# Attention on one core: the first 128 columns of W_Q and W_K split ahead of the rest, the first batch's context loaded into the accumulator, and three x transposes moved into the V products

## The chip, the cores and the metric

The kernel runs on one core of a Trainium2 chip. The metric is the device time of one execution in microseconds, here the median of three runs. A core has five engines that run side by side and meet through semaphores: TensorE (PE in the profile, its weight loads PEld), VectorE (DVE), ScalarE (ACT), GpSimd (POOL) and SyncE (SP), which here issues every DMA.

## The reference

Two layers of gated attention and feed-forward work over x of 8 batches of 512 rows by 512 columns, in float32. Only the first part, the attention of layer 0, is touched:

```
q = layernorm(x) @ W_Q + b_Q ; k = ctx @ W_K + b_K ; v = ctx @ W_V + b_V     (16 heads of 32)
out = softmax(q k^T / sqrt(32)) v ;  x = x + tanh(g) * (out @ W_O + b_O)
```

After it come a feed-forward part with ternary weights (their codes are made during the attention), a second attention without projections, and a product with block-quantised weights (W_ffn of layer 1, quantised during the attention too).

## The kernel before

All of the change is in `attention_phase`. Each engine runs its own instruction list. The lists come from one clock: steps are entered with a tick (`ck.add(tick, rank, name, ...)`), a batch has 640 ticks, and every engine walks the steps in the order of their ticks (ACT and DVE with small extra delays by kind of step), unrolled over the 8 batches. A tick sets the order only; the time is set by what waits for what.

A batch has 4 groups of 160 ticks, one for each 4 heads. A group is 16 slots of 8 ticks, then a burst. In a slot PE does one `max` product (a query tile's scores, of which DVE takes the row maximum, L870) and one `score` product (scores again, with the maximum's row appended, of which ACT takes the exponential, L751). In the burst PE does the 16 products with V (`pv`, L643) and the column sums (`den`, L662); then DVE takes four reciprocals (`recip`, L881) and the normalised output (L886), in the slots of the next group. PE may run at most two `max` products ahead of DVE.

Between these go the fillers, which make the next batch ready:

- `t`: a tile of normalised x or of the context is transposed on PE (four 128x128 transposes, L566); ACT writes a rounded high part (L701), then DVE the low part (L845). x goes to `xt`, the context to `ct`. Tiles 0 to 3 are x, tiles 4 to 7 the context.
- `qk`: four chunks of three products for one group of 128 columns and one side (Q or K), L582, then ACT (L714) and DVE (L857) write the two parts with the bias. `spill` and `fill` carry them by DMA to the layout of `stack`; the part of group 0's K goes there directly.
- `v`: sixteen chunks of three products (L596) in the slots of a batch's own group 0, and ACT reads out each of the four results (L735).

The results of `t`, `qk` and `v` share two PSUM banks, `work`, which go round in the order of the ticks (`Turns`): each user waits until the user before the last has been read out.

Before, `tx_at = (0, 1.5, 3, 4.5)` and `tc_at = (10.8, 12.3, 13.8, 15.3)` put all eight transposes into group 1 (slots counted from its start), the chunks of `(0, Q)` at slots 6 to 9.45 of it, and those of `(0, K)` at 16.8 to 20.25, which is the start of group 2. A context tile is loaded into the `stage` slot that its x tile leaves, six ticks after that tile's transposes.

At the start SP loads four x tiles, then all of W_Q, the biases, all of W_K, later W_V. Each weight is written as a high part by ACT (`split_weight`, L671) and a low part by DVE (L825), 2048 elements per partition in one instruction each, W_Q's on ACT between the third and the fourth normalisation (L723). W_V's low part is made by POOL (`ones_row`, L939). The block quantisation of the layer 1 weight is a series of steps on DVE (`quantise`, L797 to L819).

Of the kernel before, what the change touches and what calls it, by code (L numbers as in the profile page):

```python
# [5 lines left out]
ALU = mybir.AluOpType  # L6
# [3 lines left out]
P = 128  # L10
# [167 lines left out]
def attention_phase(nc, NB, keep0, keep1, x, ctx_in, w_q, b_q, w_k, b_k, w_v, b_v, spill, attn_t, ctx_t, ffn_w, w_o, b_o, weight, delta_w,  # L178
# [54 lines left out]
    with ExitStack() as ctx:  # L233
# [14 lines left out]
        def permuted(n, h):  # L248

            to = w["qkv"[n]][:, :, h, :]  # L250
            src = probs[:, n].rearrange("p a b -> p (a b)").rearrange("p (c e) -> p c e", c=C)
            if n == 2:
                return to, src
            return (to.rearrange("p c (g r j) -> p c g r j", g=G, j=J), src.rearrange("p c (g j r) -> p c g r j", g=G, j=J))
# [36 lines left out]
        w_loaded, w_hi, w_lo = [sem(f"w_loaded_{n}") for n in "qkv"], sem("w_hi"), sem("w_lo")  # L291
        wv_lo, bias_put, bias_turned, bias_done, ln_nmean = sem("wv_lo"), sem("bias_put"), sem("bias_turned"), sem("bias_done"), sem("ln_nmean")
        consts, bias_loaded, pool_consts = sem("consts"), sem("bias_loaded"), sem("pool_consts")
        loaded = [sem(f"loaded{i}") for i in range(STAGE)]
# [126 lines left out]
        def stage_wait(engine, it, shift, i):  # L421
            wait_count(engine, loaded[i % STAGE], it, shift, 2 * T // STAGE, i // STAGE + 1, 16)

        with nc.Block() as block:
            @block.sync
            def _(sp):
# [10 lines left out]
                def load_weight(n, src):  # L437
                    sp.dma_start(probs[:, n], src.rearrange("(c p) e -> p c e", p=P)).then_inc(w_loaded[n], 16)

                def window(it, shift, name, args):  # L440
                    b = it + shift
                    if name == "load":
                        i, = args
                        sync_wait(sp, held, t_full, it, shift, 2 * T, i - STAGE + 1)
                        src = x if i < T else ctx_in
                        sp.dma_start(stage[:, i % STAGE, :], src[bass.ds(b, 1), (i % T) * P:(i % T + 1) * P, :])\
                            .then_inc(loaded[i % STAGE], 16)
# [91 lines left out]
            def _(pe):  # L539
# [15 lines left out]
                def window(it, shift, name, args):  # L555
                    if name == "t":
# [8 lines left out]
                        for c in range(C):  # L565
                            last = nc.tensor.transpose(turns.bank("t", i)[:, c * P:(c + 1) * P],  # L566
                                                       stage[:, i % STAGE, c * P:(c + 1) * P], ident[:])
                        last.then_inc(t_full, 1)
                    elif name == "qk":
                        g, side, c = args  # L570
                        if c == 0:
                            if isinstance(it, int) and it + shift == 0 and g == 0:
                                pe.wait_ge(w_hi, side + 1)
                                pe.wait_ge(w_lo, side + 1)
# [11 lines left out]
                    elif name == "v":  # L586
                        i, c = args
                        if c == 0:
                            if isinstance(it, int) and it + shift == 0 and i == 0:
                                pe.wait_ge(w_hi, 3)  # L590
# [76 lines left out]
            def _(act):  # L667
                def split_weight(n):
                    act.wait_ge(w_loaded[n], 16)
                    to, at_n = permuted(n, HI)  # L670
                    nc.scalar.activation(to, at_n, ACT.Copy).then_inc(w_hi, 1)  # L671
# [17 lines left out]
                def window(it, shift, name, args):  # L689
                    if name == "t":  # L690
# [12 lines left out]
                        if isinstance(it, int) and it + shift == 0 and i == T - 1:  # L703
                            put_biases()
                            split_weight(1)
                    elif name == "qk" and args[2] == C - 1:
# [9 lines left out]
                        if isinstance(it, int) and it + shift == 0 and g == 0 and side == K:  # L716
                            split_weight(2)
                            small_tables()
                    elif name == "norm":
# [5 lines left out]
                        if isinstance(it, int) and it + shift == 0 and i == T - 2:  # L725
                            split_weight(0)
                        if it + shift == 0 and i == T - 1:
                            act.wait_ge(bias_loaded, 48)
                            nc.scalar.activation(bpart[:].rearrange("n (r j) -> n r j", j=J), brow[:].rearrange("n (j r) -> n r j", j=J),
                                                 ACT.Copy).then_inc(bias_put, 1)  # L730
# [51 lines left out]
            def _(dve):  # L782
# [39 lines left out]
                def split_weight(n):  # L822
                    dve.wait_ge(w_hi, n + 1)
                    (to, at_n), (high, _) = permuted(n, LO), permuted(n, HI)
                    nc.vector.tensor_tensor(to, at_n, high.bitcast(F32), ALU.subtract).then_inc(w_lo, 1)  # L825

                def window(it, shift, name, args):
                    if name == "ln1":
# [9 lines left out]
                        if isinstance(it, int) and it + shift == 0 and i == T - 1:  # L838
                            split_weight(0)
                    elif name == "t":  # L840
# [6 lines left out]
                        if isinstance(it, int) and it + shift == 0 and i == T - 1:  # L847
                            split_weight(1)
                            dve.wait_ge(bias_done, 2)
                        if it + shift == 0 and i == 2 * T - 1:  # L850
# [3 lines left out]
                    elif name == "qk" and args[2] == C - 1:  # L854
                        g, side, _ = args
                        wait_count(dve, qk_hi, it, shift, 2 * G, 2 * g + side + 1)
                        nc.vector.scalar_tensor_tensor(part[:, side, LO, :], turns.bank("qk", g, side)[:], bias[:, side, g:g + 1],  # L857
                                                       part[:, side, HI, :].bitcast(F32), ALU.add, ALU.subtract).then_inc(qk_lo, 1)
# [67 lines left out]
            def _(pool):  # L926
# [7 lines left out]
                def ones_row():  # L934
# [3 lines left out]
                    pool.wait_ge(w_hi, 3)  # L938
# [901 lines left out]
```

## Time and profile before

| | us |
|---|---|
| runs | 1613.11 median, 1610.33 to 1617.53 |
| profiled execution, its own time | 1618.44 |
| its span | 1616.7 |
| first `max` product starts | 50.40 |
| burst of batch 0, group 0 (its `den`) | 103.78 |
| last burst of the attention (its `den`) | 837.07 |

Times in rows are microseconds from the start of the span. In a timeline row stand start, duration, engine, line, operation, tiles, shapes and count, and in brackets the idle time of the engine just before, with what ended it. A window row has its bounds, its length and each engine's busy time with its count; the windows here run from one group's `den` to the next, and the sum is over the seven groups 1 that have all their fillers. Matmul durations overlap: the distance from one start to the next is what a matmul costs in a dense stretch.

### The profile page before, as it was taken

What the parts mean: (1) busy time and instruction counts of PE and PEld (TensorE: products, weight loads), DVE (VectorE), ACT (ScalarE), POOL (GpSimd) and SP (SyncE); (2) the same over time, 40 slices, a digit from 0 to 9 for tenths busy, and PEclk for the clock granted to TensorE, in tenths of its full rate; (3) what the DMA queues carried; (4) which work ended last, traced back from release to release, by engine and by line L of the source; (5) the groups of instructions that cost most, each with busy time, mean ns of one, the idle gap of its engine ahead of it and who ended that gap; (6) DMA issues with size and microseconds to landing.
All of it is one profiled execution on the core that took longest, in us unless ns stands there. A gap on an engine that the chain in (4) does not pass through costs nothing. (4 is left out here: it accounts for less than half of the span.)

```text
span 1616.7 us, 24697 instructions
## 1 busy us (share of the span) xinstructions
PE 1479.7 (92%) x6994; PEld 939.2 (58%) x6994; DVE 1229.8 (76%) x2135; ACT 879.3 (54%) x1435; POOL 887.7 (55%) x1148
## 2 busy tenths in 40 slices
PE   4789989999999999999784999999999978999997
PEld 3565666566665565666432555555555447787785
DVE  4867687677778778786552788888888848999996
ACT  4256666666566565665442555555555535565552
POOL 2166766675775756755552343343334316777775
PEclk8889999999999989999777999999999989999998
DMA  5666858586694875957932344444444743556521
GB/s 189 170 208 182 245 160 237 170 231 193 164 275 141 223 221 145 280 137 209 268 79 62 92 113 111 108 107 107 107 110 107 192 144 125 163 167 206 165 86 62
DMA packets 233868, 261.13 MB, mean 162 GB/s; under 512 B 139804, under 2 KB 162856, under 8 KB 224040
## 3 DMA queue, kind: packets, MB, share of 16 engines
q1 hardware_dynamic: 233768, 259.95, 57.3%
q8 instruction: 44, 0.72, 0.2%
q14 instruction: 56, 0.46, 0.1%
HBM read 143.20 MB, written 78.68 MB: 137 GB/s over the span
## 5 line engine op out<-in xcount | busy, mean ns | idle before, releaser
L751 ACT ACTIVATE a_probs<-a_sc 128x512 f32<-128x512 f32 x512 | 300.3, 595 | 277.4 <-PE a_sc L624 275.3
L870 DVE TENSOR_REDUCE a_negmax<-a_mx 128x1 f32<-128x512 f32 x512 | 337.8, 674 | 96.4 <-PE a_mx L607 95.8
L965 POOL TENSOR_TENSOR a_acc<-a_acc,a_probs 128x512 f32<-128x512 f32 x248 | 311.5, 1285 | 10.6 <-ACT a_probs L751 9.4
L965 POOL TENSOR_TENSOR a_acc<-a_probs 128x512 f32<-128x512 f32 x124 | 156.8, 1284 | 239.6 <-ACT a_probs L751 238.8
L607 PE MATMUL a_mx<-a_stack 96*128 96x512 f32 x512 | 230.2, 450 | 38.5 <-DVE a_negmax L870 23.4
L1116 PE MATMUL bank<-wcode,b_xq 128*128 128x512 bf16 x1024 | 229.8, 383 | 11.1 <-DMA b_xq<-b_xcode 11.1
L624 PE MATMUL a_sc<-a_stack 97*128 97x512 f32 x512 | 215.7, 423 | 11.1 <-DMA a_stack<-a_mrow 9.7
L1116 PEld LDWEIGHTS bank<-wcode,b_xq 128*128 128x128 bf16 x1024 | 100.9, 99 | 135.2 <-DMA b_xq<-b_xcode 12.4
L881 DVE RECIPROCAL a_attn<-a_den 128x128 f32<-128x128 f32 x128 | 120.7, 947 | 72.4 <-PE a_den L662 57.1
L607 PEld LDWEIGHTS a_mx<-a_stack 96*128 96x128 f32 x512 | 102.7, 201 | 113.8 <-DVE a_negmax L870 57.9
L1154 ACT ACTIVATE b_sig<-bank,b_tok 128x512 f32<-128x512 f32 x128 | 87.4, 683 | 94.5 <-PE bank L1116 91.4
L582 PE MATMUL a_work<-a_xt,k_wbuf 128*128 128x512 f32 x384 | 123.6, 437 | 12.0 <-DVE a_xt L845 12.0
L1208 DVE TENSOR_TENSOR b_hid<-b_sig,bank 128x512 f32<-128x512 f32 x128 | 87.4, 685 | 51.3 <-ACT b_sig L1154 51.3
L624 PEld LDWEIGHTS a_sc<-a_stack 97*128 97x128 f32 x512 | 103.2, 202 | 37.8 <-DMA a_stack<-a_mrow 10.0
L643 PE MATMUL a_pvb<-a_probs,a_v 128*32 128x512 f32 x1024 | 119.9, 607 | 0.7 <-ACT a_probs L751 0.7
L1158 ACT ACTIVATE b_hid<-b_hid,b_htok 128x2048 f32<-128x2048 f32 x32 | 64.1, 2003 | 102.9 <-DVE b_htok L1227 102.9
L582 PE MATMUL a_work<-k_wo,k_wbuf 128*128 128x512 f32 x384 | 115.1, 412 | 1.5 <-DVE k_wo L845 1.5
L1105 PE MATMUL bank<-k_wo,b_apart 128*128 128x512 f32 x384 | 102.6, 417 | 14.9 <-POOL b_apart L1259 13.9
L1123 PE MATMUL bank<-wcode,b_hq 128*128 128x512 bf16 x512 | 116.1, 380 | 0.0
L596 PE MATMUL a_work<-k_wbuf,k_wo 128*128 128x512 f32 x384 | 111.2, 401 | 0.0
L1530 PE MATMUL bank<-c_ct,c_xt 128*128 128x512 f32 x384 | 98.9, 407 | 11.1 <-DVE c_xt L1628 8.8
L582 PEld LDWEIGHTS a_work<-a_xt,k_wbuf 128*128 128x128 f32 x384 | 80.9, 214 | 35.1 <-issue 14.2
(169 smaller groups left out, 2573.5 us busy)
## 6 DMA issues: line engine op xcount, KB each, us to landing
a_stack<-spill SPq DMA_DIRECT2D x168, 256.0 KB, 7.2
spill<-k_part SPq DMA_DIRECT2D x56, 512.0 KB, 3.4
ctx_t<-k_wo SPq DMA_DIRECT2D x16, 1024.0 KB, 11.1
c_ct<-ctx_t SPq DMA_DIRECT2D x8, 2048.0 KB, 8.2
a_stage<-in_x_dram SPq DMA_DIRECT2D x32, 256.0 KB, 5.1
a_stage<-in_ctx_dram SPq DMA_DIRECT2D x32, 256.0 KB, 3.3
a_wsum<-in_L_ffn_w_gate_dram SPq DMA_DIRECT2D x8, 1024.0 KB, 5.9
attn_t<-a_attn SPq DMA_DIRECT2D x32, 256.0 KB, 4.5
```

Of the source, the lines that this page charges most:

```text
L582: last = nc.tensor.matmul(turns.bank("qk", g, side)[:], w["qk"[side]][:, c, a, g * P:(g + 1) * P], src[:, c, m, :], start=c == 0 and n == ...
L596: last = nc.tensor.matmul(turns.bank("v", i)[:], ct[:, c, a, i * P:(i + 1) * P], w["v"][:, c, m, :], start=c == 0 and n == 0, stop=c == C ...
L607: nc.tensor.matmul(mx[i % 2][:], stack[0:96, g, Q, j, t * P:(t + 1) * P], stack[0:96, g, K, j, :], start=True, stop=True).then_inc(mx_full, 1)
L624: nc.tensor.matmul(sc[i % 2][:], stack[0:97, g, K, j, k * P:(k + 1) * P], stack[0:97, g, Q, j, :], start=True, stop=True).then_inc(s_full, 1)
L643: last = nc.tensor.matmul(pvb[DH * j:DH * (j + 1), :], v[:, k, h * DH:(h + 1) * DH], probs[:, k, j, :], start=k == 0, stop=k == T - 1)
L751: nc.scalar.activation(probs[:, k, j, :], sc[i % 2][:], ACT.Exp, scale=SCALE).then_inc(exp_done, 1)
L870: nc.vector.tensor_reduce(negmax[:, g % 2, j, t:t + 1], mx[i % 2][:], axis=AX.X, op=ALU.max, negate=True).then_inc(mx_done, 1)
L881: nc.vector.reciprocal(attn[:, g % 2, q * P:(q + 1) * P], den[:, q * P:(q + 1) * P]).then_inc(recip_done, 1)
L965: nc.gpsimd.tensor_tensor(acc[:, j], probs[:, 0, j] if k == 1 else acc[:, j], probs[:, k, j], ALU.add)\
L1105: last = nc.tensor.matmul(bank_o[:], apart[:, t % 2, a, c, :], wo[:, c, m, :], start=c == 0 and n == 0, stop=c == C - 1 and n == 2)
L1116: last = nc.tensor.matmul(bank[:], xq[:, t % 2, c, :], gu_code[:, side * M + m, :, c, :], start=c == 0, stop=c == C - 1)
L1123: last = nc.tensor.matmul(bank_d[:], hq[:, t % 2, r, :], wcode[:, 2 * M:3 * M, r, :], start=r == 0, stop=r == R - 1)
```

## The change

What it does:

1. `tx_at` becomes (-7.25, -3.5, -0.5, 0.3): x tiles 0 to 2 are transposed in the slots of group 0, at ticks 70, 100 and 124 of it, between the V chunks, and tile 3 at tick 2 of group 1. The loads of the context follow by six ticks.
2. `(0, Q)` moves to slots 2.6 to 6.05 of group 1, the context transposes to 7.5, 9, 10.5 and 12, and `(0, K)` to 13.4 to 16.85: three of its four chunks come ahead of the burst of group 1. The fills of group 0 move from slots 17 and 22.8 to 16 and 19.4.
3. The first batch's context tiles are loaded into `acc` (not in use by then), without waiting for `stage`.
4. W_Q and W_K are loaded and split in two parts, columns 0 to 127 (all that group 0 needs) and 128 to 511, the latter in four instructions of 384 elements per partition on ACT and on DVE. The order at the start changes: no split stands between the normalisations any more.
5. The first quantisation steps (`quantise` 0 to 2) move on DVE from the last context tile to the K part of group 0, behind the split of the rest of W_K.

```diff
+        SPLIT_AT = (1, 2, 2 + C, 2 + 2 * C, 3 + 2 * C)
+        def pieces(n, h, cols):
+            to, src = w["qkv"[n]][:, :, h, cols], staged(n, cols)
             if n == 2:
-                return to, src
+                return [(to, src)]
+            to, src = to.rearrange("p c (g r j) -> p c g r j", r=DH, j=J), src.rearrange("p c (g j r) -> p c g r j", r=DH, j=J)
+            if cols.stop == P:
+                return [(to[:, :, 0], src[:, :, 0])]
+            return [(to[:, c], src[:, c]) for c in range(C)]
...
-        tx_at, tc_at = (0, 1.5, 3, 4.5), (10.8, 12.3, 13.8, 15.3)
-        qk_at = {(0, Q): 6, (0, K): 16.8, (1, Q): 21.4, (1, K): 26, (2, Q): 30.6, (2, K): 35.2, (3, Q): 39.8, (3, K): 44.4}
-        fill_at = {(0, Q): 17, (0, K): 22.8, (1, Q): 32, (1, K): 37, (2, Q): 44.5, (2, K): 49.5, (3, Q): 52, (3, K): 56}
+        tx_at, tc_at = (-7.25, -3.5, -0.5, 0.3), (7.5, 9, 10.5, 12)
+        qk_at = {(0, Q): 2.6, (0, K): 13.4, (1, Q): 21.4, (1, K): 26, (2, Q): 30.6, (2, K): 35.2, (3, Q): 39.8, (3, K): 44.4}
+        fill_at = {(0, Q): 16, (0, K): 19.4, (1, Q): 32, (1, K): 37, (2, Q): 44.5, (2, K): 49.5, (3, Q): 52, (3, K): 56}
@@ SP, load @@
-                        sync_wait(sp, held, t_full, it, shift, 2 * T, i - STAGE + 1)
+                        to = stage[:, i % STAGE, :]
+                        if b == 0 and i >= T:
+                            to = acc[:, i - T, :]
+                        else:
+                            sync_wait(sp, held, t_full, it, shift, 2 * T, i - STAGE + 1)
...
-                        if isinstance(it, int) and b == 0 and i == T - 1:
-                            load_weight(0, w_q)
+                        if b == 0 and i == T - 1:
+                            load_weight(0, w_q, slice(0, P), w_first[0])
                             load_biases()
-                            load_weight(1, w_k)
-                        if isinstance(it, int) and b == 0 and i == 2 * T - 1:
+                        if b == 0 and i == 2 * T - 1:
+                            load_weight(1, w_k, slice(0, P), w_first[1])
+                            load_weight(0, w_q, slice(P, D))
+                            load_weight(1, w_k, slice(P, D))
                             load_weight(2, w_v)
@@ ACT, t @@
-                        if isinstance(it, int) and it + shift == 0 and i == T - 1:
+                        if it + shift == 0 and i == 1:
+                            split_weight(0, True)
+                        if it + shift == 0 and i == T - 2:
+                            act.wait_ge(bias_loaded, 48)
+                            nc.scalar.activation(bpart[:].rearrange("n (r j) -> n r j", j=J), brow[:].rearrange("n (j r) -> n r j", j=J),
+                                                 ACT.Copy).then_inc(bias_put, 1)
+                        if it + shift == 0 and i == T - 1:
                             put_biases()
-                            split_weight(1)
+                        if it + shift == 0 and i == 2 * T - 2:
+                            split_weight(1, True)
+                        if it + shift == 0 and i == 2 * T - 1:
+                            split_weight(0, False)
@@ ACT, qk @@
-                        if isinstance(it, int) and it + shift == 0 and g == 0 and side == K:
-                            split_weight(2)
+                        if it + shift == 0 and g == 0 and side == K:
+                            split_weight(1, False)
+                            split_weight(2, False)
                             small_tables()
@@ DVE, qk; its low parts of the splits stand at the same tiles as ACT's high parts @@
+                        if it + shift == 0 and (g, side) == (0, K):
+                            split_weight(1, False)
+                        if it + shift == 0 and (g, side) == (0, K):
                             dve.wait_ge(q_loaded, 16)
                             for n in range(3):
                                 quantise(n)
```

## Rows read from the trace of the kernel before

**Rows 1.** The page: busy time, share and instructions of each engine.

```profile
PE 1479.7 (92%) x6994; PEld 939.2 (58%) x6994; DVE 1229.8 (76%) x2135; ACT 879.3 (54%) x1435; POOL 887.7 (55%) x1148
```

**Rows 2.** Group 1 windows: busy PE, PEld, DVE, ACT, POOL; clock, DMA share, GB/s.

```profile
199.98:224.87 24.89, 21.62 (x121) 13.52 (x117) 19.34 (x30) 16.18 (x31) 15.07 (x12) 0.93 0.35 117
...
sum 182.16, PE 159.77 PEld 100.24 DVE 145.75 ACT 112.43 POOL 105.36; mean PE 22.82 PEld 14.32 DVE 20.82 ACT 16.06 POOL 15.05
```

**Rows 3.** Window, same columns: the group 0 before it, `den` to `den`.

```profile
176.53:199.98 23.45, 23.45 (x126) 16.27 (x122) 14.58 (x21) 15.36 (x28) 16.20 (x16) 1.00 0.90 270
```

**Rows 4.** Waits of PE, 100 to 780 us: total, times, longest.

```profile
PE a_mx L607 <- issue: 9.6, 10, 1.7
```

**Rows 5.** Timeline of PE in one group 1.

```profile
200.95 0.66 PE L566 MATMUL a_work<-k_ident,a_stage 128*128 128x128 f32 x4
201.36 0.48 PE L607 MATMUL a_mx<-a_stack 96*128 96x512 f32 x1
...
205.91 0.50 PE L607 MATMUL a_mx<-a_stack 96*128 96x512 f32 x1 [1.27 <-DVE a_negmax L870]
...
209.19 0.94 PE L582 MATMUL a_work<-a_xt,k_wbuf 128*128 128x512 f32 x3 [1.64 <-DVE a_xt L845]
...
212.23 0.63 PE L607 MATMUL a_mx<-a_stack 96*128 96x512 f32 x1
```

**Rows 6.** Timeline of DVE in the same group.

```profile
206.96 0.95 DVE L881 RECIPROCAL a_attn<-a_den 128x128 f32<-128x128 f32 x1
...
207.83 0.63 DVE L870 TENSOR_REDUCE a_negmax<-a_mx 128x1 f32<-128x512 f32 x1
...
208.37 0.68 DVE L845 TENSOR_TENSOR a_xt<-a_work,a_xt 128x512 fp32r<-128x512 f32 x1
208.96 0.69 DVE L870 TENSOR_REDUCE a_negmax<-a_mx 128x1 f32<-128x512 f32 x1
```

**Rows 7.** Timeline of the end of a group 0, ACT and PE.

```profile
191.38 0.60 ACT L735 ACTIVATE a_v<-a_work 128x512 f32<-128x512 f32 x1
...
191.65 1.55 PE L596 MATMUL a_work<-k_wbuf,k_wo 128*128 128x512 f32 x6
...
196.52 3.64 PE L643 MATMUL a_pvb<-a_probs,a_v 128*32 128x512 f32 x32
...
196.81 0.57 ACT L735 ACTIVATE a_v<-a_work 128x512 f32<-128x512 f32 x1
```

**Rows 8.** Timeline of group 2, SP and PE.

```profile
232.93 1.94 SPq L480 DMA_DIRECT2D a_stack<-k_part  x3
...
241.12 0.47 PE L607 MATMUL a_mx<-a_stack 96*128 96x512 f32 x1 [0.81 <-issue]
```

**Rows 9.** Timeline of the start, all engines.

```profile
9.44 0.19 POOL L955 TENSOR_TENSOR a_nbias<-a_nmean,a_rstd 128x1 f32<-128x1 f32 x1
...
9.87 3.77 ACT L671 ACTIVATE k_wbuf<-a_probs 128x2048 fp32r<-128x2048 f32 x1 [0.18 <-DMA a_probs<-in_L_xattn_W_Q_dram]
...
22.12 5.03 PE L582 MATMUL a_work<-a_xt,k_wbuf 128*128 128x512 f32 x12 [1.50 <-DVE a_xt L845]
...
34.88 2.28 DVE L797 TENSOR_REDUCE a_attn<-a_wsum 128x64 f32<-128x2048 f32 x1
...
41.20 0.75 DVE L857 SCALAR_TENSOR_TENSOR k_part<-a_work,a_bias,k_part 128x512 fp32r<-128x512 f32 x1 [3.59 <-ACT k_part L714]
42.11 2.02 SPq L480 DMA_DIRECT2D a_stack<-k_part  x3
...
43.12 4.55 POOL L939 TENSOR_TENSOR k_wbuf<-a_probs,k_wbuf 128x2048 fp32r<-128x2048 f32 x1 [26.50 <-ACT k_wbuf L671]
...
44.96 2.78 DVE L803 SCALAR_TENSOR_TENSOR a_attn<-a_attn 128x64 f32<-128x64 f32 x1
...
50.40 0.76 PE L607 MATMUL a_mx<-a_stack 96*128 96x512 f32 x1 [5.09 <-DMA a_stack<-k_part]
...
51.20 0.69 DVE L870 TENSOR_REDUCE a_negmax<-a_mx 128x1 f32<-128x512 f32 x1 [0.54 <-PE a_mx L607]
```

More of the change, by code:

```diff
@@ L289, in attention_phase @@
         pvb, den = pb("pvb"), pb("den")
[L291 removed]
+        w_loaded, w_first, w_hi, w_lo = [sem(f"w_loaded_{n}") for n in "qkv"], [sem(f"w_first_{n}") for n in "qk"], sem("w_hi"), sem("w_lo")
         wv_lo, bias_put, bias_turned, bias_done, ln_nmean = sem("wv_lo"), sem("bias_put"), sem("bias_turned"), sem("bias_done"), sem("ln_nmean")
         consts, bias_loaded, pool_consts = sem("consts"), sem("bias_loaded"), sem("pool_consts")
[L294 removed]
+        loaded, ctx_first = [sem(f"loaded{i}") for i in range(STAGE)], [sem(f"ctx_first{i}") for i in range(T)]
         ln_stats, ln_mv, ln_eps, ln_rstd, ln_bias, ln_done = (sem(n) for n in ("ln_stats", "ln_mv", "ln_eps", "ln_rstd", "ln_bias",
@@ L421, in stage_wait @@
         def stage_wait(engine, it, shift, i):
-            wait_count(engine, loaded[i % STAGE], it, shift, 2 * T // STAGE, i // STAGE + 1, 16)
+            b = it + shift
+            if b == 0 and i >= T:
+                engine.wait_ge(ctx_first[i - T], 16)
+            else:
+                engine.wait_ge(loaded[i % STAGE], 16 * (2 * b + i // T + (b == 0)))
         with nc.Block() as block:
@@ L565, in window @@
                         for c in range(C):
-                            last = nc.tensor.transpose(turns.bank("t", i)[:, c * P:(c + 1) * P],
-                                                       stage[:, i % STAGE, c * P:(c + 1) * P], ident[:])
+                            tile = acc[:, i - T] if it + shift == 0 and i >= T else stage[:, i % STAGE]
+                            last = nc.tensor.transpose(turns.bank("t", i)[:, c * P:(c + 1) * P], tile[:, c * P:(c + 1) * P], ident[:])
                         last.then_inc(t_full, 1)
@@ L571, in window @@
                         if c == 0:
-                            if isinstance(it, int) and it + shift == 0 and g == 0:
-                                pe.wait_ge(w_hi, side + 1)
-                                pe.wait_ge(w_lo, side + 1)
+                            if it + shift == 0 and g <= 1:
+                                pe.wait_ge(w_hi, SPLIT_AT[2 * g + side])
+                                pe.wait_ge(w_lo, SPLIT_AT[2 * g + side])
+                            if it + shift == 0 and g == 0:
                                 pe.wait_ge(bias_done, 2)
@@ L667, in _, with split_weight @@
             def _(act):
[L668 to L671, printed above, removed]
+                def split_weight(n, first):
+                    cols = slice(0, P) if first else slice(P, D)
+                    if n == 2:
+                        cols = slice(0, D)
+                    act.wait_ge(w_first[n] if first else w_loaded[n], 16)
+                    for to, at_n in pieces(n, HI, cols):
+                        nc.scalar.activation(to, at_n, ACT.Copy).then_inc(w_hi, 1)
                 def small_tables():
@@ L724, in window @@
                                              bias=nbias[:, i:i + 1]).then_inc(ln_done, 1)
[L725 to L730, printed above, removed]
                     elif name == "v" and args[1] == C - 1:
@@ L820, in quantise, with split_weight @@
                     ins.then_inc(q_step, 1)
[L822 to L825, printed above, removed]
+                def split_weight(n, first):
+                    dve.wait_ge(w_hi, SPLIT_AT[n if first else n + 2])
+                    cols = slice(0, P) if first else slice(P, D)
+                    for (to, at_n), (high, _) in zip(pieces(n, LO, cols), pieces(n, HI, cols)):
+                        nc.vector.tensor_tensor(to, at_n, high.bitcast(F32), ALU.subtract).then_inc(w_lo, 1)
                 def window(it, shift, name, args):
@@ L853, in window @@
                                 quantise(n)
[L854 to L858, printed above, removed]
                         if it + shift == 0 and (g, side) == (1, Q):
```

36 lines of the change are left out of this document (21 added, 15 removed).

## The prediction

> **What bounds the kernel now.** The page first: PE is busy 92% of the span, DVE 76% [rows 1], so time is lost where PE waits, and I looked for that inside the attention (to 837 us). The windows by group come next. A group 0, with sixteen V chunks, takes 23.45 us with PE busy for all of them at full clock [rows 3]: PE bound. A group 1 takes 24.89 us at best and 182.16 / 7 = 26.0 us on average, though it has fewer chunks, with PE busy 22.8 of 26.0 and DVE 20.8 [rows 2]. The timelines say why. All eight tiles' low parts, four reciprocals and sixteen row maxima go through DVE; PE waits 1.27 us for a maximum and 1.64 us for the last x tile [rows 5], and soon after that the products last 0.63 us: the granted clock falls to 1.2 GHz. At a mean clock of 0.93 that is 2 x 0.07 x 24.89 = 3.5 us at the lower level, which costs 1.7 us if PE is busy throughout; it isn't quite, and I take 1.5. Without it this group 1 would take 24.89 - 1.5 = 23.4, so the seven lose 26.0 - 23.4 = 2.6 us each, mostly to the clock. Each group 2 has a wait of 0.8 us for the fill of K's group 0, seven such among the ten of [rows 4], one in [rows 8].
>
> So x and the first Q chunks are a real stall; the question is whether moving them ends it, and what it costs in group 0, where PE has nothing to spare.
>
> **Group 0: what is added.** Three tiles' transposes move in. One costs PE 201.36 - 200.95 = 0.4 us [rows 5], and there is no cover: 1.2 us. Then the two banks. With x tile 0 between V2 and V3, V3 now takes the bank of V2 and waits for ACT to read it. V2's read-out is 191.38 to 191.98, and V3's first chunk started at 191.65 [rows 7]: with the semaphore 0.4 us late. x tile 2 (tick 124) takes the bank of V3, and all of the burst is queued behind it. V3 is read out only from 196.81 to 197.38, behind the maximum's row and an exponential on ACT, while the burst started at 196.52 [rows 7]: 0.9 us late. Sum: 1.2 + 0.4 + 0.9 = +2.5 us. Bounds: +1.2 (the read-outs come earlier) to +3.0. ACT and DVE take these tiles inside PE's 1.17 us slots and in the burst, where DVE is idle: nothing.
>
> **Group 1: what goes and what replaces it.** DVE works back to back here, at intervals of 207.83 - 206.96 = 0.87 us for a reciprocal, 0.54 to 0.6 for a maximum, 0.6 for a low part [rows 6]. In the new order the low part of context tile 7 stands behind 4 reciprocals (3.5), 13 maxima (7.8), 4 other low parts and itself (3.0), Q's part (0.65) and the output (0.6): 15.6, with 0.4 of start and gap makes 16.0 us after the burst. `(0, K)` can't start before. Then come three chunks at 0.7, two slots at 0.47 and the row of maxima's transpose at 0.2: 19.3 us to the next burst. Before it was 221.41 - 200.95 = 20.5 with the clock's 1.5 in it, 19.0 without. So with the same loss by the clock: +0.3. The stall moves from Q behind x to K behind the context.
>
> Does the clock still fall? Before, in the 8.24 us ahead of the late Q chunk, PE issued seven slots and four transposes, 3.3 + 1.6 = 4.9 us of work. In the new order the stretch from 8 to 16 us holds six slots and four transposes, 2.8 + 1.6 = 4.4 of 8. It is no denser, so I keep the fall and its mean price of 2.6 us, now over K's chunks and the burst. Bounds: -2.3 (gone; +0.3 - 2.6) to +2.
>
> **Group 2.** Three of K's chunks leave its start, 2.1 us of PE work. DVE there has four reciprocals, some ten maxima, K's part and the output in the first 9.6 us before (3.5 + 6.0 + 0.65 + 0.6 = 10.7, less the maxima that end later), so PE would only wait for it: I take 0.2 of the 2.1. K's fill, before issued at 232.93, 8.1 us after the burst, with the product that needs it waiting until 241.12 (8.2 us from issue), is now issued about 4 us after it, as K's part comes early and its step stands at tick 27 in place of 54: the 0.8 us wait goes whole. Sum -1.0. Bounds: -2.1 to +0.7, the last where the clock falls a second time: after the one K chunk PE now has only four slots, 1.9 of 3.9 us.
>
> Groups 2's later part, group 3, the last batch (which has no next batch) and everything behind the attention are as before: 0. SP's queue: the context loads come up to 10 slots earlier, each waits for its x tile, and no fill stands behind it that is due: 0.
>
> **Seven batches:** 7 x (2.5 + 0.3 - 1.0) = +12.6 us.
>
> **The start.** Two more DMAs on SP, at some 0.5 us each to issue, with the DMA engines idle later: 0. Before, the fourth normalisation waited on ACT for the end of W_Q's split, 9.87 + 3.77 = 13.6, though its value was ready at 9.44 + 0.19 [rows 9]: now it starts 3.9 us earlier. W_Q's low part (on DVE, about as long as the high part's 3.77) held the first x tile's low part up by some 2.2 us more; the new first piece costs a quarter, 0.95, on each engine: 1.2 net. So Q starts at 22.12 - 3.9 - 1.2 = 17.0. From Q to the K part's end it was 41.95 - 22.12 = 19.8; 1.1 of this was Q's low part behind W_K's on DVE, which goes: K's part ends at 35.8, six us early. The pieces between (0.95 for W_K's first, 2.9 for W_Q's rest) lie beside PE's five us of Q and K. The fill takes 50.40 - 42.11 = 8.3: the first `max` product could start at 44.3, six us early. But the maximum needs DVE, and DVE now has more in between. The rest of W_K's low part waits for ACT's four pieces (to 37.8), then 2.9 to 40.7; `quantise` 0 to 2 2.7; the next Q part 0.7; the steps 3 to 5. Those took from 44.96 to 51.20 before, but 2.78 of it is one step of 64 elements that ended at 47.74, as POOL's W_V low part ended at 47.67: it stood still behind POOL. Without that they take 0.3 + 3.4 less the wait of 0.6 for the product = 3.1. End 47.4 against 51.20: -3.8. From there to 84 us DVE is the bound, as 24 maxima and the quantisation alternate on it, so the shift is passed on.
>
> That is with DVE first. ACT ends W_V's high part at 39.8, in the third of DVE's four pieces. If POOL's 4.55 us gets in between the pieces, the fourth waits until 44.6 and the chain ends at 44.6 + 0.7 + 2.7 + 0.7 + 3.1 = 51.8: +0.6. The row of 2.78 us shows that a DVE step can stand behind POOL, none shows who wins a gap. I take the mean: -1.6, bounds -3.8 and +0.6.
>
> The Trainium skill has this as a rule (SBUF — State Buffer, section "SBUF: two separate sides"): GpSimd and a VectorE operation with two SBUF inputs lock each other out for a whole instruction, and whichever starts first has the ports. The trace agrees with the 2.78 us. By that rule the start would end 0.6 us later if POOL takes the gap and 3.8 earlier if DVE does; it doesn't say who does.
>
> **Sum.** 1618.44 + 12.6 - 1.6 = 1629.4 for an execution like the profiled one. That execution was 5.3 us above the median of 1613.11, so the median comes to 1613.1 + 11.0 = 1624.
>
> **Rivals.**
> - The clock no longer falls. For: the waits for x before the fall are gone, and Q's chunks are now dense. Against: the stretch behind them is as thin as the old one, at 4.4 of 8 us. It gives 7 x (2.5 - 2.3 - 1.0) - 1.6 = -7.2: 1606, no slower than before; with the start at -3.8 too 1604. It decides from the point where the clock stays up in five of the seven batches. 16%.
> - V's read-outs hold nothing up: ACT reads V3 before PE is at tile 2. For: ACT is not full. Against: in the rows the read-out ends 0.9 us after the burst's start. 7 x 1.3 = 9 less: 1615. 18%.
> - A second fall of the clock at the start of group 2, where DVE alone sets the pace. For: 1.9 of 3.9 us. Against: it is short. 7 x 1.7 = 12 more: 1636. 18%.
>
> My forecast, with the falls as they were and DVE and POOL as they come, has 48%, and its own range is 1617 to 1632.
>
> **How the numbers follow.** What a measurement of this kernel tells from no change is about 0.5%, 8 us: 1605 to 1621. Faster: nearly half of the first rival and a little of the others, 0.12. Within: the rest of it, most of the second, a third of my own case, 0.36. Slower: 0.52. The range is 1603 to 1641: the first rival with the best start below, the third above.
>
> **What would show it.** Right: V3's first chunk and the transposes of x tile 2 with waits of 0.4 and 0.9 us for ACT's V read-outs in each group 0, `den` to `den` near 26 there; in group 1 a wait ahead of `(0, K)` and half clock behind it; no wait for the fill in group 2; the first row maximum at 47.4 or 51.8. Wrong: group 1 below 24 us on average with the clock at full, or a group 0 below 25.

## The result, and the profile after

The changed kernel takes 1628.28 us (median of five runs, 1626.84 to 1633.27), beside 1616.12 for the kernel before on the same chip: ratio 1.0081, 95% interval 1.0057 to 1.0104. It is slower, by 12 us where 11 were forecast (the forecast started from a median of 1613.11 over three runs of the kernel before, which is 1616.12 over five). Its profiled execution took 1626.84 us with a span of 1625.0, 8.3 us more than before.

From the two traces, `den` to `den` (one profiled execution each):

| | before | after | difference |
|---|---|---|---|
| up to the first `den` | 103.78 | 106.03 | +2.25 |
| group 0 of batches 1 to 7 | 164.27 | 182.63 | +18.36 |
| group 1 of batches 0 to 6 | 182.16 | 175.38 | -6.78 |
| group 2 of batches 0 to 6 | 164.78 | 160.96 | -3.82 |
| group 3 of batches 0 to 6 | 168.70 | 168.41 | -0.29 |
| groups 1 and 2 of the last batch | 53.38 | 53.40 | 0.0 |
| behind the attention | 779.63 | 778.19 | -1.44 |

The windows of group 0, which answer to [rows 3] (busy PE, PEld, DVE, ACT, POOL; clock, DMA share, GB/s): 26.4 us in place of 23.5, six times, at full clock, and PE is idle for 1.2 of them. The last batch has no next batch to transpose and takes 24.00.

```profile
177.06:203.48 26.42, 25.19 (x137) 17.39 (x133) 16.38 (x24) 16.88 (x31) 16.21 (x16) 1.00 0.92 269
...
769.41:793.41 24.00, 23.69 (x125) 16.19 (x121) 15.65 (x23) 14.21 (x24) 15.12 (x12) 1.00 1.05 276
```

The timeline of PE (durations overlap, the distance between starts is the cost) and of ACT in the same stretch, against [rows 7]. V0 to V3 are the four V results of a group 0, of four chunks each. V3's first chunk waits for ACT's read-out of V2, and x tile 2 for that of V3:

```profile
189.39 0.60 PE L584 MATMUL a_work<-k_ident,a_stage 128*128 128x128 f32 x4
189.75 0.47 PE L625 MATMUL a_mx<-a_stack 96*128 96x512 f32 x1
...
192.39 0.40 PE L642 MATMUL a_sc<-a_stack 97*128 97x512 f32 x1
193.10 1.64 PE L614 MATMUL a_work<-k_wbuf,k_wo 128*128 128x512 f32 x6 [0.31 <-ACT a_v L761]
...
198.14 0.40 PE L642 MATMUL a_sc<-a_stack 97*128 97x512 f32 x1
199.47 0.63 PE L584 MATMUL a_work<-k_ident,a_stage 128*128 128x128 f32 x4 [0.92 <-ACT a_v L761]
200.02 3.64 PE L661 MATMUL a_pvb<-a_probs,a_v 128*32 128x512 f32 x32
```

```profile
192.36 0.60 ACT L761 ACTIVATE a_v<-a_work 128x512 f32<-128x512 f32 x1
...
198.75 0.57 ACT L761 ACTIVATE a_v<-a_work 128x512 f32<-128x512 f32 x1
```

A `score` product costs 0.23 in a dense stretch, so V3 was due at 192.62 and x tile 2 at 198.37: 0.5 and 1.1 us late. The transposes cost 0.44 each with what they delay behind them, 0.55 the last.

Group 1, against [rows 2]: two windows and the sum. Where the granted clock stays at 1.00 (2.4 GHz throughout) the group takes 24.4, where it shows 0.93 (2 x 0.07 x 25 = 3.5 us at 1.2 GHz) 25.0 to 25.3 (the fourth batch, with more matmuls, 25.0 at 1.00). Before, no group 1 was at 1.00 and five were at 0.87 or below. Part of the -6.8 us is scatter between executions: with the old ticks the seven groups 1 take 182.16 in the kernel before but 176.99 and 177.90 in experiments 2 and 10, with the new ones 175.38 in the changed kernel and 172.73 and 172.90 in experiments 1 and 4.

```profile
106.03:131.32 25.29, 22.83 (x118) 13.88 (x114) 17.64 (x27) 15.19 (x28) 15.08 (x12) 0.93 0.32 110
203.48:227.91 24.43, 21.27 (x119) 12.61 (x115) 17.60 (x27) 14.87 (x28) 15.02 (x12) 1.00 0.27 89
...
sum 175.38, PE 156.18 PEld 94.94 DVE 132.71 ACT 103.65 POOL 105.50; mean PE 22.31 PEld 13.56 DVE 18.96 ACT 14.81 POOL 15.07
```

Its inside, PE's timeline against [rows 5]. Q's chunks wait only 0.23. The second context tile waits for Q's part, the products for two maxima, and `(0, K)` for the low part of the last context tile, 16.7 us after the group's first product; the burst comes 20.0 after it.

```profile
204.45 0.50 PE L625 MATMUL a_mx<-a_stack 96*128 96x512 f32 x1
...
207.18 0.93 PE L600 MATMUL a_work<-a_xt,k_wbuf 128*128 128x512 f32 x3 [0.23 <-DVE a_xt L871]
...
214.31 0.63 PE L584 MATMUL a_work<-k_ident,a_stage 128*128 128x128 f32 x4 [0.48 <-DVE k_part L884]
...
216.61 0.50 PE L625 MATMUL a_mx<-a_stack 96*128 96x512 f32 x1 [1.05 <-DVE a_negmax L903]
...
221.13 0.93 PE L600 MATMUL a_work<-k_wo,k_wbuf 128*128 128x512 f32 x3 [0.48 <-DVE k_wo L871]
...
224.45 3.64 PE L661 MATMUL a_pvb<-a_probs,a_v 128*32 128x512 f32 x32
```

Group 2 takes 22.3 at full clock and 23.5 at 0.93, which four of the seven show. Before, all seven were at 1.00 and took 23.5 to 23.6. The fill's wait of [rows 8] is gone; where DVE sets the pace at the opening there is now one of 1.32 us for a maximum.

```profile
227.91:250.21 22.30, 20.98 (x111) 12.98 (x107) 17.62 (x28) 13.88 (x25) 15.29 (x14) 1.00 0.75 201
325.06:348.56 23.50, 22.19 (x111) 14.12 (x106) 17.87 (x28) 13.87 (x25) 15.59 (x15) 0.93 0.71 189
```

```profile
233.40 0.50 PE L625 MATMUL a_mx<-a_stack 96*128 96x512 f32 x1 [1.32 <-DVE a_negmax L903]
```

PE's waits between 100 and 780 us, against [rows 4]: the `issue` waits fall from 9.6 to 3.7 us, and the four new lines (V's read-out twice, K's first chunk for the context's low part, a tile for Q's part) hold 6.5 + 3.9 + 3.4 + 1.8 = 15.6, where 8.8 of x's 10.5 are gone. The waits for a row maximum grow as well, from 15.3 to 22.0. Two lines of the kernel before, then the changed one:

```profile
PE a_mx L607 <- DVE a_negmax L870: 15.3, 28, 1.3
PE a_work L582 <- DVE a_xt L845: 10.5, 7, 1.6
...
PE a_mx L625 <- DVE a_negmax L903: 22.0, 30, 1.3
PE a_work L584 <- ACT a_v L761: 6.5, 7, 0.9
PE a_work L600 <- DVE k_wo L871: 3.9, 7, 0.7
PE a_mx L625 <- issue: 3.7, 4, 1.0
PE a_work L584 <- DVE k_part L884: 3.4, 7, 0.5
PE a_work L614 <- ACT a_v L761: 1.8, 6, 0.3
PE a_work L600 <- DVE a_xt L871: 1.7, 7, 0.3
```

The start, against [rows 9]. Q's first chunk is 3.7 us earlier and the fill of K's part 5.6, and there the lead stops: four DVE pieces that take 3.02 us with POOL held back (experiment 4) take 7.21, because POOL's low part of W_V got in between. PE, whose next chunks read these pieces, waits 7.71 us, and the first row maximum is at 52.30, 1.1 us later than before.

```profile
18.39 5.43 PE L600 MATMUL a_work<-a_xt,k_wbuf 128*128 128x512 f32 x12 [1.50 <-DVE a_xt L871]
...
36.54 2.02 SPq L497 DMA_DIRECT2D a_stack<-k_part  x3
...
38.82 7.21 DVE L853 TENSOR_TENSOR k_wbuf<-a_probs,k_wbuf 128x384 fp32r<-128x384 f32 x4 [2.43 <-ACT k_wbuf L693]
...
40.73 4.70 POOL L972 TENSOR_TENSOR k_wbuf<-a_probs,k_wbuf 128x2048 fp32r<-128x2048 f32 x1 [24.15 <-ACT k_wbuf L693]
...
46.13 4.18 PE L600 MATMUL a_work<-k_wo,k_wbuf 128*128 128x512 f32 x9 [7.71 <-issue]
...
49.26 0.21 DVE L829 SCALAR_TENSOR_TENSOR a_attn<-a_attn 128x64 f32<-128x64 f32 x1
...
52.30 1.28 DVE L903 TENSOR_REDUCE a_negmax<-a_mx 128x1 f32<-128x512 f32 x2
```

### The profile page after: what moved, and what is told of

Same layout as the page of the kernel before. It is cut to its first block and busy times, and to the rows that moved or that the text cites. A ratio compares the mean times of both kernels' runs of the same rounds, so it can differ in the third digit from the quotient of the medians.

```text
span 1625.0 us, 24720 instructions
## 1 busy us (share of the span) xinstructions
PE 1478.2 (91%) x6994; PEld 932.6 (57%) x6994; DVE 1230.6 (76%) x2143; ACT 882.2 (54%) x1443; POOL 888.4 (55%) x1148
## 5 line engine op out<-in xcount | busy, mean ns | idle before, releaser
L600 PE MATMUL a_work<-a_xt,k_wbuf 128*128 128x512 f32 x384 | 116.2, 415 | 3.7 <-DVE a_xt L871 3.2
L1563 PE MATMUL bank<-c_ct,c_xt 128*128 128x512 f32 x384 | 99.0, 407 | 10.8 <-DVE c_xt L1661 8.5
L1298 POOL TENSOR_TENSOR b_nmean<-b_mv,k_minus 128x1 f32<-128x1 f32 x32 | 6.1, 190 | 172.1 <-DVE b_mv L1213 172.1
```

The lines of the kernel that those rows point to most:

```text
L600: last = nc.tensor.matmul(turns.bank("qk", g, side)[:], w["qk"[side]][:, c, a, g * P:(g + 1) * P], src[:, c, m, :], start=c == 0 and n == ...
L1563: last = nc.tensor.matmul(bank_s[t % 2][:], xt[:, t % R2, c, a, :], ct[h][:, c, m, :], start=c == 0 and n == 0, stop=c == C - 1 and n == 2)
```

## The experiments

Each ratio is to the kernel before on the same chip, with its 95% interval. Unless said otherwise the edit is to the changed kernel.

### 1 and 2: the ticks without the start, the start without the ticks

The first puts the three new lines of ticks into the kernel before; the second puts the old ones back into the changed kernel.

```diff
-        tx_at, tc_at = (0, 1.5, 3, 4.5), (10.8, 12.3, 13.8, 15.3)
+        tx_at, tc_at = (-7.25, -3.5, -0.5, 0.3), (7.5, 9, 10.5, 12)
...
```

> The kernel before with the new ticks alone (tx_at, tc_at, qk_at, fill_at); the start as before. My theory: the steady state carries the loss. From the trace of the changed kernel: group 0 with x tiles +3.0 us for seven batches (21), group 1 -1.0 each (7), group 2 -0.5 each (4), so +10 us: ratio 1.006, and the first row maximum stays at 51.2. Rival, the new start carries it: ratio 1.000.

> The changed kernel with the ticks of before: first columns first, the first context in acc, splits in pieces. My theory: +1 us, as POOL's W_V low part stands between DVE's pieces and the first row maximum is at 52.3 in place of 51.2: ratio 1.0005. Rival, the start carries the loss: ratio 1.006. Second rival, the earlier loads and Q help more than DVE's first maximum shows: ratio 0.997.

The ticks alone: 1.0073 (1.0051 to 1.0094), with seven groups 0 of 182.61 us in all. The start alone: 0.9998 (0.9984 to 1.0013). Their product is 1.0071, within the interval of the whole. So the loss is in the ticks, and by the trace in group 0. The start is worth nothing that can be told; there POOL got in between DVE's pieces as well (7.22 us), with the first row maximum at 50.46.

### 3: x tile 1 next to tile 0

Tile 1 now comes just ahead of V3's first chunk and not behind it. It takes V2's bank, V3 takes tile 0's and tile 2 takes tile 1's, so that nothing ahead of the burst waits for V3's read-out.

```diff
-        tx_at, tc_at = (-7.25, -3.5, -0.5, 0.3), (7.5, 9, 10.5, 12)
+        tx_at, tc_at = (-7.25, -4.875, -0.5, 0.3), (7.5, 9, 10.5, 12)
```

> The changed kernel with x tile 1 at tick 89 of group 0 in place of 100, just ahead of V3. Now V3 shares its bank with x tile 0, and x tile 2 with x tile 1, so neither waits for ACT to read a V; tile 1 itself waits for V2 (0.3 us). My theory: group 0 falls by the 1.3 us wait of tile 2 less 0.3, from 26.4 to about 25.3, seven times: 7 to 8 us less than the changed kernel, ratio to before 1.003. Rival, the wait only moves (the burst then waits for V's read-out or for POOL's sums): ratio 1.008 as for the changed kernel.

1.0003 (0.9987 to 1.002): the whole loss is gone, which is more than was expected. Group 0 takes 25.25 in the six batches with tiles and 23.47 in the last. Of the waits in it one is left, V2's read-out, now on tile 1:

```profile
191.22 0.63 PE L584 MATMUL a_work<-k_ident,a_stage 128*128 128x128 f32 x4 [0.31 <-ACT a_v L761]
```

That saves 182.63 - 174.97 = 7.7 us over the seven windows, and 1.0 more before the first `den`. In the profiled pair another part stands in groups that the edit doesn't touch: six of seven groups 1 and five of seven groups 2 stay at full clock, against two and three in the changed kernel, 3.5 and 2.3 us less. That the moved tile does this isn't shown. With the same ticks in groups 1 and 2, nine windows are below 1.00 in the changed kernel, seven in experiment 1 and five in experiment 4, all three without the move; with it three here and five in experiment 5. And the twelve runs of this one kernel differ as much: the fastest, 1612.94, had a mean granted clock of 0.965, the slowest, 1622.74, one of 0.957. The two ratios differ by 0.0078, 12.6 us, but the intervals are 8 and 5 us wide, so the direct 8.7 us may be all of it.

```profile
200.42:224.84 24.42, 21.25 (x118) 12.61 (x114) 17.60 (x27) 14.86 (x29) 15.02 (x12) 1.00 0.26 88
...
488.52:513.40 24.88, 22.58 (x118) 13.87 (x114) 21.24 (x32) 15.29 (x26) 15.07 (x12) 0.93 0.44 138
```

### 4: POOL's low part behind DVE's four pieces

```diff
+                    pool.wait_ge(w_lo, SPLIT_AT[3])
```

> The changed kernel with one wait more: POOL starts W_V's low part only when DVE has done all four pieces of W_K's rest. My theory: the pieces take 3 us in place of 7.2, the first row maximum comes at 48 in place of 52.3, and as DVE is the bound up to 84 us all of it is passed on: 4 us less than the changed kernel, ratio to before 1.0055. Rival, PE at half clock is the bound there, or V's first chunks now wait for POOL: ratio 1.008.

1.0068 (1.0042 to 1.0095), against 1.0081 without the wait; the two intervals overlap, and both the expected 1.0055 and the rival's 1.008 lie within. The pieces took 3.02, but the first row maximum came at 50.74, 1.6 us earlier and not the four expected: another DVE step stood behind POOL, one of 64 elements, while the reduction of 2048 elements beside it took its usual 2.27.

```profile
39.06 3.02 DVE L853 TENSOR_TENSOR k_wbuf<-a_probs,k_wbuf 128x384 fp32r<-128x384 f32 x4 [2.44 <-ACT k_wbuf L693]
42.00 2.27 DVE L823 TENSOR_REDUCE a_attn<-a_wsum 128x64 f32<-128x2048 f32 x1
42.25 4.59 POOL L973 TENSOR_TENSOR k_wbuf<-a_probs,k_wbuf 128x2048 fp32r<-128x2048 f32 x1 [25.76 <-DVE k_wbuf L853]
44.30 2.58 DVE L825 TENSOR_SCALAR a_attn<-a_attn 128x64 f32<-128x64 f32 x1
```

### 5: POOL behind the first quantisation steps, on the kernel of 3

```diff
+                    pool.wait_ge(q_step, 6)
```

> As e3 (x tile 1 with tile 0), and POOL starts W_V's low part only when DVE has done the quantisation's step 5, so that no DVE step of the start stands behind it. e4 showed why the wait for the split alone gave half: a quantisation step of one input and 64 elements then took 2.58 us behind POOL. My theory: the pieces 3.0 us, that step 0.2 us, the first row maximum at about 48 in place of 51.6, and 3.5 us less than e3: ratio 0.998. Rival: PE's half clock there sets the pace, and nothing is passed on: 1.000.

0.999 (0.9976 to 1.0003), which tells the expected 0.998 from the rival's 1.000 as little as this kernel from experiment 3. The first row maximum is at 46.31 and the first `den` at 102.29, against 51.63 and 105.06 in experiment 3: of 5.3 us 2.8 reach the `den`. They are lost again in this execution, as three groups 1 fall below full clock and the seven take 176.38 for 171.88. The block has moved once more, to the next DVE step that reads and writes SBUF alone (0.42 us without POOL, 3.89 here), and PE waits 3.65 us for the maximum behind it:

```profile
46.57 4.55 POOL L973 TENSOR_TENSOR k_wbuf<-a_probs,k_wbuf 128x2048 fp32r<-128x2048 f32 x1 [29.99 <-DVE a_wsum L833]
...
47.51 3.89 DVE L835 TENSOR_SCALAR a_wsum<-a_wsum 128x512 f32<-128x512 f32 x1
...
53.17 0.79 PE L625 MATMUL a_mx<-a_stack 96*128 96x512 f32 x1 [3.65 <-DVE a_negmax L903]
```

### 6: context and `(0, K)` back where they were, on the kernel of 3

Of the lines `qk_at` and `fill_at` only the entries that change are given.

```diff
-        tx_at, tc_at = (-7.25, -4.875, -0.5, 0.3), (7.5, 9, 10.5, 12)
+        tx_at, tc_at = (-7.25, -4.875, -0.5, 0.3), (10.8, 12.3, 13.8, 15.3)
...
-(0, K): 13.4, fill 19.4
+(0, K): 16.8, fill 22.8
```

> As e3, but the context's transposes, K's group 0 and its fill at the places of before (10.8 to 15.3, 16.8 to 20.25, 22.8): only x and Q are early. My theory: DVE bounds group 1, and K's three chunks ahead of the burst come behind its last low part, so they are no gain there. Without them the burst comes when DVE has done some 14 maxima, 5 low parts, 4 reciprocals, Q's part and the output, at 17 in place of 20.0 us: group 1 from 24.4 to 21.6, group 2 from 22.3 back to 23.5, with its 0.8 us wait for the fill. 7 x 1.6 = 11 us less than e3, ratio 0.9935. Rival, K early is a gain: group 1 stays at 24 and group 2 loses 1.2: 8 us more than e3, ratio 1.005.

0.997 (0.9955 to 0.9984). At full clock group 1 takes 22.0 (21.6 was expected), but five of the seven aren't at full clock, and 162.1 - 7 x 22.0 = 8 us of the 18 that it could gain over experiment 3 are lost, most of them so. That the clock falls because the stretch ahead of the context has no filler now is argued, not shown. Group 2 is back at 23.5. So at full clock `(0, K)` ahead of the burst costs 2.4 us in group 1 and gives back 1.2 in group 2.

```profile
200.64:224.37 23.73, 21.93 (x110) 13.26 (x106) 17.70 (x27) 15.51 (x28) 15.02 (x12) 0.86 0.26 90
296.47:318.48 22.01, 19.26 (x109) 10.90 (x101) 17.69 (x27) 14.82 (x28) 14.90 (x12) 1.00 0.27 96
```

### 7: x tile 2 out of group 0, on the kernel of 3

```diff
-        tx_at, tc_at = (-7.25, -4.875, -0.5, 0.3), (7.5, 9, 10.5, 12)
+        tx_at, tc_at = (-7.25, -4.875, 0, 1.2), (7.5, 9, 10.5, 12)
```

> As e3, but x tile 2 back in group 1 (slot 0, tile 3 at 1.2): two x tiles in group 0. My theory: PE bounds group 0 and DVE group 1, so group 0 gets back 0.44 us and group 1 gives 0.6 for the low part ahead of K: 1 us more than e3 in all, ratio 1.001. Rival, a tile among the V chunks is the dear one: 3 us less, 0.998.

1.0028 (1.0007 to 1.0048); the interval overlaps that of experiment 3, the windows decide. Group 0 gains the 0.44 us (24.81), but a group 1 takes 25.2 at full clock in place of 24.4, and one at 0.82 takes 28.34. A tile costs more where DVE is the bound than where PE is.

### 8: reciprocals of 8 columns in place of 128

This kernel leaves out the softmax's division in batches 1 to 7: each reciprocal covers 8 columns and the output is scaled by a constant (`to` ends 8 columns on; both lines of code are shortened). One run.

```diff
-nc.vector.reciprocal(attn[:, g % 2, q * P:(q + 1) * P], den[:, q * P:(q + 1) * P])
+nc.vector.reciprocal(attn[:, g % 2, q * P:to], den[:, q * P:to])
...
-nc.vector.tensor_tensor(attn[:, g % 2, :], pvb[:], attn[:, g % 2, :], ALU.mult)
+nc.vector.tensor_scalar(attn[:, g % 2, :], pvb[:], 0.002, None, ALU.mult)
```

> The changed kernel with the reciprocals of batches 1 to 7 over 8 columns in place of 128, and the output scaled by a constant: a look at DVE as the bound (the softmax's normalisation is left out). My theory: 3 us of DVE's work leave each group, so group 1 falls from 24.4 to about 22 us, group 2's opening has no wait of 1.3 us and the group takes about 21 to 22, the clock does not fall in either, and group 0 stays at 26.4, as PE and the bank waits bound it. Rival, the waits in group 1 are for ACT or the banks: group 1 stays within 0.5 us of 24.4.

Refuted for group 1: with 2.3 us of DVE's work gone it still takes 24.3. In group 2 the wait at the opening goes, and it takes 21.3 for 22.3. And as expected no group 1 or 2 of batches 0 to 6 has a fall of the clock, where the changed kernel has nine: with less work on DVE between PE's products the clock stayed up, in one execution. The run took 1616.64 us.

```profile
203.55:227.87 24.32, 20.61 (x118) 12.74 (x114) 15.26 (x27) 14.76 (x28) 15.01 (x12) 1.00 0.24 89
```

PE's timeline says why. The first context tile is transposed at 212.45, in the changed kernel at 212.48 (8.9 and 9.0 us after `den`), right behind PE's own products and Q's chunks. The next tile needs the bank of Q's result, so it waits for Q's part, and from there four low parts, six maxima and the output follow on DVE until K's first chunk.

```profile
212.45 0.60 PE L584 MATMUL a_work<-k_ident,a_stage 128*128 128x128 f32 x4
...
214.29 0.63 PE L584 MATMUL a_work<-k_ident,a_stage 128*128 128x128 f32 x4 [0.78 <-DVE k_part L884]
...
221.10 0.93 PE L600 MATMUL a_work<-k_wo,k_wbuf 128*128 128x512 f32 x3 [0.50 <-DVE k_wo L871]
```

### 9 to 12: combinations

All four have the edit of 5, which puts POOL last, and share the runs of the kernel before. Number 9 adds the ticks of 6, number 10 those of the kernel before, number 11 those of 3 with `(0, K)` and its fill as in 6, and number 12 is 9 with one more edit (again the entries alone):

```diff
-(0, K): 16.8, fill 22.8
+(0, K): 16, fill 21.2
```

> e6 and e5 together: x tiles 0 to 2 in group 0 with tile 1 beside tile 0, Q early, the context and K at the places of before, and POOL's W_V low part behind the quantisation's step 5. The first burst came 2.8 us earlier in e5 than in e3, with the ticks the same; if the start is independent of the ticks, this is 2.8 us less than e6: ratio 0.9953. Rival, the gain of the start is taken back by the clock or by the fills: 0.997.

> e2 (the new start with the ticks of before) and POOL's W_V low part behind step 5. My theory: the new start itself is sound and only lost its gain to POOL's operation between DVE's: 2.8 us less than e2, ratio 0.998. Rival: it has no gain with the ticks of before: 1.000.

> As e9, but the context's transposes at 7.5 to 12 as in the changed kernel; K stays behind the burst. e6 moved the two together; this tells them apart. e8 showed that the second half of group 1 is a chain of its own: PE's last Q chunk, the bank's read-out, then DVE without a gap until K starts. My theory: K ahead of the burst is the dear part, and group 1 is at 22.2 us here where the clock doesn't fall, against 22.0 in e6 and 24.4 in e3: ratio 0.996. Rival, the dense context transposes are: group 1 at 24, ratio 1.003.

> As e9, but K's chunks 0.8 slots earlier (16 to 19.45, still behind the burst) and its fill at 21.2 in place of 22.8. My theory: DVE writes K's part about 1 us earlier, the fill lands before its product is due, and the 0.8 us wait of each group 2 goes: 5 us less than e9, ratio 0.992. Rival, the wait goes but DVE, which sets the pace at the opening of group 2, gives it back: 0.995.

| | ratio | 95% |
|---|---|---|
| 9 | 0.9975 | 0.996 to 0.999 |
| 10 | 0.9973 | 0.9957 to 0.9989 |
| 11 | 0.9957 | 0.994 to 0.9974 |
| 12 | 0.9952 | 0.9935 to 0.9969 |

Number 10 has the old ticks and POOL last, and the kernel gains 4.4 us; without POOL's wait (experiment 2) it gained 0.3. But the traces don't put this gain at the start. The first `den` is at 102.23, 1.6 us earlier than before and 1.3 later than in experiment 2 (100.93). The rest stands in windows whose ticks are the same: the seven groups 1 take 177.90 for 182.16 before, and against experiment 2 it is groups 3 of batches 0 to 6, 168.93 for 175.78. So the gain is clear in the runs, and its place is open.

Number 9 (0.9953 expected, outside its interval) is no better than 10: x tiles in group 0 and x tiles in group 1 come out level. Number 11 tells apart the two moves that 6 took together: with the context early and `(0, K)` behind the burst, a group 1 at full clock takes 22.27, as in its expectation, and not the rival's 24; so it is `(0, K)` ahead of the burst that costs. In 12, where 0.992 was expected, the fill did not come in time: its step stands earlier, but it is issued at 232.10, 7.9 us behind `den` (8.1 in number 9), as K's last chunk runs behind the burst, and the wait is still there:

```profile
240.27 0.47 PE L625 MATMUL a_mx<-a_stack 96*128 96x512 f32 x1 [0.82 <-issue]
```

So what 12 has over 9 isn't shown to be more than scatter; the intervals overlap. Number 12 has the lowest ratio, 0.9952; 10 to 12 can't be told apart. All four beat the kernel before and the changed one.

## Why the prediction was right, step by step

The forecast was 1624 within 1603 to 1641, and 1628.28 was measured, with the mechanism it named in group 0. Terms missed in opposite directions, and that the total came within about 1 us of the forecast, by the medians, is in part luck: in seven batches group 1 was 8.9 us lower than its term, group 2 3.2 higher, group 0 0.9 higher, and the stretch up to the first `den` 3.9 higher.

**Group 0, forecast +2.5, measured +2.97.** The step held, wait by wait: 1.2 for the transposes measured 1.4, 0.4 for V3's bank 0.5, 0.9 for x tile 2 1.1. A transposition's price had been taken as the distance to the next product; that product too starts its successor some 0.08 later (0.31 in place of 0.23). Experiments 1 and 3 show the cause: with the ticks alone the seven groups 0 take the same 182.61 us, and moving one tile by 1.375 slots takes 1.2 us out of each with tiles. The multiplication by seven was a little too much at the end: the last of the seven windows, 24.00, has no tiles (batch 0's tiles are in the stretch before the first `den`, which is at 106.75 in experiment 1, 3.0 later than before, and which the forecast gave no tiles). That the 24.00 is not the 23.47 of before and of experiment 3 fits a turn of the banks that is kept also where no tile is transposed.

**Group 1, forecast +0.3, measured -1.0.** The order's part was under-priced: `(0, K)` at 16.7 and not at 16.0, the burst at 20.0 and not at 19.3, so 24.4 at full clock where 23.7 followed from the forecast. The term that failed is the clock's. "I keep the fall and its mean price of 2.6 us" was the step; the falls stayed in five of seven batches but were short, and a group at 0.93 costs 0.6 to 0.9 more than one at 1.00. The sum: +0.3 + 0.7 - 2.0 = -1.0. The 2.6 of before is itself an estimate, as no group 1 of it ran at full clock, and it was taken from an execution whose groups 1 were 4 to 5 us longer in all than in experiments 2 and 10 with the same ticks.

The reason given for 16 us was wrong in its make-up. It was a sum of DVE's work from the burst, reciprocals first; experiment 8 takes 2.3 us of that away and K's chunk doesn't move. The chain in the trace is PE's order up to the last of Q's chunks, then Q's part through ACT and DVE, which frees the bank for the second context tile, then DVE.

**Group 2, forecast -1.0, measured -0.55.** Without a fall it is 23.54 - 22.3 = -1.2, with the fill's wait gone as stated. The third rival, a second fall in this group, came true in four of seven batches at 1.2 us each, 0.7 on average. So the clock's cost is 0.6 in group 1 and 0.7 in group 2, where it was put at 2.6 in group 1 alone.

**The start, forecast -1.6 as a mean of -3.8 and +0.6.** The branch with POOL in the gap came true: 51.8 forecast for the first row maximum, 52.30 measured (Q's first chunk 1.4 later than 17.0). The branch with DVE first had its price right too, but not by the ordering it named: experiment 4, with POOL behind the pieces, gave 50.74 for 47.4, because the next one-input step stood still instead. Only with POOL behind the first six quantisation steps is it at 46.3 to 47.5. The step that failed here is "so the shift is passed on": the first row maximum moved by -0.7, -4.5 and -5.3 us (experiment 2 and 10 against before, 5 against 3), the first `den` by -2.9, -1.6 and -2.8.

The block is told by the Trainium skill (SBUF — State Buffer, section "SBUF: two separate sides"): GpSimd and certain VectorE operations shut each other out for a whole instruction, and the one that starts first has the ports. The traces agree: of the steps that overlapped POOL's 4.5 us, the two-input ones in SBUF and the one-input L825 and L835 stood still, the reduction out of SBUF and the maxima out of PSUM did not. The page names a performance mode for one-input operations; that L825 and L835 ran in it isn't visible in a trace.

**In total** for the seven batches: forecast +12.6, measured 18.4 - 6.8 - 3.8 = +7.8 in the windows, to which the first group 0 adds 3.0 before the first `den`: +10.8. With what is left of the start (2.25 - 3.0 = -0.7), group 3's -0.3 and the unchanged stretch behind the attention, -1.4, the spans differ by 8.3; the medians differ by 12.2, so the profiled pair shows less than the runs, and 4 us of the median's difference have no place in a trace here.

**What stays open.** Why the same group 1 falls to 1.2 GHz in one batch and not in the next: windows of equal work stand at 1.00 and at 0.93, and runs of one kernel differ in their mean granted clock (0.957 to 0.966 in experiment 3, the slower runs with the lower clock in the main). In experiments 1, 2, 6, 7, 8 and 11 one to three groups 3 of batches 3 to 5 take 26.7 to 30.0 us, with waits of PE of up to 4.2 us behind no recorded releaser; the kernels before and after don't show it, with either set of ticks others do, and its cause was not tried. A profiled pair can differ by 7 us through these windows alone, more than most effects here. Why the first `den` doesn't follow the first row maximum is open too (102.23 in 10, 100.93 in 2, whose first maximum is 3.8 us later).

## What to carry to other kernels

A filler moved from a stretch where PE waits to one where PE has nothing to spare costs its full time, and more if it shares buffers that go round: count the turn of the bank for every user behind it, and move the tile to where the turn is free. A wait placed on one engine to keep it out of another's way can just move the collision, as both places tried here did, to the next instruction that stands still behind it, so look for a stretch where none comes. Price the clock as a separate term with its own range, and don't read a change of a few us from one pair of profiles: windows with the same instruction order differ by as much from execution to execution. A gain at one point of the start need not reach the next; look where it ends.

## What the runs showed of the hardware

- A POOL instruction that became ready during four DVE instructions issued back to back got in between them in all six traces that have the pieces and no wait on POOL (7.21 to 7.23 us for the four, in the changed kernel and experiments 2, 3, 6, 7 and 8; 3.02 or 3.03 with POOL held back). A DVE step of 64 elements can then stand for the rest of POOL's 4.6 us (2.58 for 0.20, experiment 4), while a reduction of 2048 elements beside it takes its usual 2.27.
- The falls of the granted clock vary between executions and kernels with the same order in those groups: nine, seven and five windows of groups 1 and 2 below 1.00 (changed kernel, experiments 1 and 4), three and five with one tile moved in group 0 (experiments 3 and 5), one profile each. In the changed kernel and experiment 3 the windows at 0.93 are 0.5 to 1.3 us longer than their like at 1.00, with some 3.5 us of each at 1.2 GHz.
